# A graph-attention layer with LayerNorm: two broadcasts and the means moved on TensorE, PSUM banks swapped, the prologue reordered

## The reference

```python
h = einsum('bnd,ade->bane', x, W);  th = tanh(h)
attn = th @ w_src + swap(th @ w_dst)            # a score for each pair of nodes and head
attn = where(attn >= 0, attn, 0.2 * attn)
attn = where(adj, attn, -999.0);  attn = softmax(attn)
feat = elu(merge_heads(attn @ h + b))
gate = sigmoid(x @ H_w.T + H_b)
out = layernorm(x + gate * feat + (1 - gate) * x)
```

## Time and profile before

| | |
|---|---|
| median of 3 runs | 798.93 us (798.83 to 800.71) |
| the profiled execution | 799.27 us |
| its span in the trace | 797.5 us |
| PE busy | 724.3 us (91%) |
| DVE busy | 711.0 us (89%) |
| POOL busy | 536.8 us (67%) |
| ACT busy | 374.9 us (47%) |
| the chain that ended last | PE 89%, ACT 3%, DVE 3% |

### The profile page before, as it was taken

How to read it: one execution, slowest core, us unless ns; L and a number is a source line. 1 busy time by engine, 2 the same in 40 slices (tenths; PEclk the granted TensorE clock), 3 DMA queues, 4 the chain that set the end, 5 groups by cost and what they waited for, 6 DMA issues and landing times.

```text
span 797.5 us, 12614 instructions
## 1 busy us (share of the span) xinstructions
PE 724.3 (91%) x3472; PEld 401.5 (50%) x3472; DVE 711.0 (89%) x1277; ACT 374.9 (47%) x804; POOL 536.8 (67%) x380
## 2 busy tenths in 40 slices
PE   4299999999999999999999999999999999999970
PEld 4164564646456464645646454564545455553430
DVE  6668899989989998998999899898989999899885
ACT  4123426355553636555363645536264563626352
POOL 7964386775949677693957769395876939584500
PEclk9599999999999999999999999999999999999995
DMA  5020021112112111211211121211202121110202
GB/s 172 0 94 1 2 91 40 54 41 93 41 50 81 39 53 39 92 39 58 73 39 53 39 92 39 72 59 39 56 36 92 39 85 47 40 24 30 79 1 79
DMA packets 32875, 43.82 MB, mean 55 GB/s; under 512 B 1234, under 2 KB 26580, under 8 KB 32852
## 3 DMA queue, kind: packets, MB, share of 16 engines
q1 hardware_dynamic: 24660, 31.35, 12.5%
q10 hardware_dynamic: 8192, 12.19, 4.2%
HBM read 30.95 MB, written 12.58 MB: 55 GB/s over the span
## 4 chain that ended last, share of the span: by engine, by line
PE 89%; ACT 3%; DVE 3%; issue 2%; POOL 2%; DMA 1%; ACTq 0%; POOLq 0%; DVEq 0%; SPq 0%
PE out_T L798 47%; PE hg L726 27%; PE vb L782 7%; PE tr L806 6%; ACT att_T L400 1%; POOL th_w L257 1%; PE hg L767 1%; PE hg L772 1%; DMA ew<-in_W 1%; DVE ew L592 1%; DVE ex L684 0%; DMA out<-y 0%; PE hg L753 0%; ACT y L433 0%; DVE w_lo L510 0%
## 5 line engine op out<-in xcount | busy, mean ns | idle before, releaser
L592 DVE SCALAR_TENSOR_TENSOR ew<-vb,u,adj_in 128x512 f32<-128x512 f32 x768 | 536.1, 742 | 22.7 <-PE vb L782 22.7
L798 PE MATMUL out_T<-ew,vals 128*64 128x512 f32 x1536 | 392.3, 603 | 1.3 <-DVE ew L592 1.3
L257 POOL TENSOR_TENSOR th_w<-th,score_w 128x768 f32<-128x768 f32 x64 | 134.6, 2105 | 184.0 <-ACT th L371 147.9
L798 PEld LDWEIGHTS out_T<-ew,vals 128*64 128x64 f32 x1536 | 114.0, 136 | 200.6 <-issue 136.2
L400 ACT ACTIVATE att_T<-out_T,tiny 128x512 f32<-128x512 f32 x96 | 66.1, 689 | 245.7 <-PE out_T L798 245.7
L726 PE MATMUL hg<-w_hi,xT_hi 128*128 128x384 f32 x384 | 150.9, 393 | 14.4 <-DVE xT_lo L515 10.4
L726 PE MATMUL hg<-w_lo,xT_hi 128*128 128x384 f32 x384 | 130.2, 339 | 0.0
L726 PE MATMUL hg<-w_hi,xT_lo 128*128 128x384 f32 x384 | 88.5, 338 | 0.0
L726 PEld LDWEIGHTS hg<-w_hi,xT_hi 128*128 128x128 f32 x384 | 74.0, 193 | 25.2 <-issue 23.7
L806 PE MATMUL tr<-ident,att_T 128*128 128x128 f32 x384 | 59.1, 277 | 21.6 <-ACT att_T L400 21.6
L782 PE MATMUL vb<-v_T,head_sel 128*128 128x512 bf16 x192 | 74.4, 390 | 0.7 <-ACT v_T L392 0.7
(11 more groups left out here) (94 smaller groups left out, 718.8 us busy)
## 6 DMA issues: line engine op xcount, KB each, us to landing
xT_in<-in_xT SPq DMA_DIRECT2D x16, 768.0 KB, 4.6
x_in<-in_x SPq DMA_DIRECT2D x16, 768.0 KB, 4.5
out<-y ACTq DMA_DIRECT2D x15, 768.0 KB, 3.5
adj_in<-in_adjT SPq DMA_DIRECT2D x16, 256.0 KB, 4.8
ew<-in_W SPq DMA_DIRECT2D x1, 576.0 KB, 4.2
ew<-in_HwT SPq DMA_DIRECT2D x1, 576.0 KB, 8.0
score_w<-in_w_rows SPq DMA_DIRECT2D x1, 384.0 KB, 6.8
out<-y SPq DMA_DIRECT2D x1, 384.0 KB, 2.5
```

Source lines behind the costliest of these rows:

```text
L257: g.tensor_tensor(th_w[:, c % 2], th[:, c].unsqueeze(1).broadcast_to([P, 2, D]), score_w[:], ALU.mult).then_inc(S["thw_done"], 1)
L592: ve.scalar_tensor_tensor(out=ew[:, (2 * C * j + i) % SLOTS, :], in0=VB[h % 4][:], scalar=u[:, q, c, h:h + 1], in1=adj_in[:, q, c, :], op0 ...
L798: te.matmul(OUT[VW * k:VW * k + VW, :], vals[:, q, c, h, :], ew[:, t % SLOTS, :], start=(c == 0), stop=(c == C - 1)).then_inc(S["ew_free"], 1)
```

## The change

- On PE, the broadcasts of the heads 0 and 1 of the next batch leave attend 5 and stand ahead of it, behind transpose_out 4. Its eight matmuls stand together.
- The means of batch b move from the next step to the turn of the step, between transpose_v(b+1) and transpose_out 4, and wait for the last gate of b. In the last step they stand there too.
- On ACT, `copy_out(b, 4)` comes ahead of `copy_vT(b+1)`.
- The banks of HG are swapped: features 0 to 2 and gate 0 use HG[0], features 3, the other gates and the means HG[1]. The waits that guard them follow.
- ACT makes the tanh first and then the copy; what waits for a free bank now waits for the copy.
- In every product, the three high-by-high matmuls come first, then the three high-by-low, then the three low-by-high (before, the first two kinds took turns).
- Prologue: the products of batch 0 wait for each part when it is used, not for all at the start. DVE does its own weighing for batch 0. The zeros of `vals` are halved between DVE (at its start) and POOL. POOL does add_bias, then split_low of batch 1, then values, and then the two sums of `add_rows`, which were a part of `add_bias`.

```diff
@@ banks
-        G_BANK = [HG[1], HG[0], HG[1], HG[1]]
+        G_BANK = [HG[0], HG[1], HG[1], HG[1]]
-        mean_ps = HG[0][:, 0:D]
+        mean_ps = HG[1][:, 0:D]
-            return HG[0] if c == 3 else HG[1]
+            return HG[1] if c == 3 else HG[0]
@@ POOL before()
+                g.memset(vals[:, 1], 0.0).then_inc(S["pool_setup"], 1)
                 pool.wait_ge(S["pool_setup"], SETUP)
-                pool.wait_ge(S["ld_cols"], 16)
-                for c in range(C):
-                    weigh(0, c)
-                add_bias(0, 0)
+                add_bias(0)
+                for c in range(C):
+                    split_low(1, 1, c)
+                pool.wait_ge(S["dve_setup"], DVE_SETUP)
                 values(0, 0)
-                for c in range(C):
-                    split_low(1, 1, c)
+                add_rows(0, 0)
@@ ACT features(b, c)
-                a.activation(h_sb[:, c], feature_bank(b, c)[:, 0:D], ACT.Copy).then_inc(S["hcopy_done"], 1)
+                if isinstance(b, int) and b == 1:
+                    act.wait_ge(S["hb_sum_done"], 1)
                 if not isinstance(b, int) or b:
                     act.wait_ge(S["thw_done"], C * (b - 1) + c + 1)
                 a.activation(th[:, c], feature_bank(b, c)[:, 0:D], ACT.Tanh).then_inc(S["th_done"], 1)
+                a.activation(h_sb[:, c], feature_bank(b, c)[:, 0:D], ACT.Copy).then_inc(S["hcopy_done"], 1)
@@ ACT step
+                copy_out(b, 4)
                 if not last:
                     copy_vT(b + 1, 1 - q)
-                copy_out(b, 4)
@@ DVE before()
+                ve.memset(vals[:, 0], 0.0).then_inc(S["dve_setup"], 1)
...
-                ve.memset(vals[:], 0.0).then_inc(S["dve_setup"], 1)
...
                 for c in range(C):
+                    dve.wait_ge(S["th_done"], c + 1)
+                    ve.tensor_tensor(th_w[:, c % 2], th[:, c].unsqueeze(1).broadcast_to([P, 2, D]), score_w[:],
+                                     ALU.mult).then_inc(S["thw_done"], 1)
                     head_sums(0, c)
@@ PE products
                 for k in range(KD):
-                    mms += [(xT_hi[:, q, k, n], w_hi[:, k, col:col + D]), (xT_hi[:, q, k, n], w_lo[:, k, col:col + D])]
+                    mms.append((xT_hi[:, q, k, n], w_hi[:, k, col:col + D]))
+                for k in range(KD):
+                    mms.append((xT_hi[:, q, k, n], w_lo[:, k, col:col + D]))
@@ PE features of batch 0
+                    products(feature_bank(b, c), q, c, 0, [],
+                             {KD: (S["w_lo_done"], 1), 2 * KD: (S["xlo_done"], c + 1)}).then_inc(S["h_done"], 1)
@@ PE step
-                if not first:
-                    pe.wait_ge(S["vT_done"], b + 1)
-                    means(b - 1, 1 - q)
...
                 if not last:
                     transpose_v(b + 1)
+                means(b, q)
                 transpose_out(b, 4)
-                attend(b, q, 5, last)
+                if not last:
+                    broadcast_v(b + 1, 1 - q, 0)
+                    broadcast_v(b + 1, 1 - q, 1)
+                attend(b, q, 5)
```

66 lines of the change are left out of this document (37 added, 29 removed).

## The result

| | before | after |
|---|---|---|
| median | 798.9 us (798.83 to 800.71) | 766.1 us (763.75 to 767.3, 4 runs) |
| ratio of the medians, with its 95% interval | | 0.9581 (0.9551 to 0.9611) |
| the profiled execution | 799.27 us | 764.97 us |
| its span | 797.5 us | 763.2 us |
| DVE busy | 711.0 us (89%) | 711.3 us (93%) |

The forecast of the median was 768.1. The two spans differ by 34.3 us, where 30.8 were forecast. DVE has as much work as before; only its waits have gone.

A forecast was written before the change was run, and what follows sets the result against it. PE and DVE, almost side by side and waiting for each other at the turn between steps, bound the kernel. Turns 25.7 us plus prologue 5.1 make 30.8 us, from 798.93 to a median of 768.1 us; range 761 to 780.

The forecast's parts named there:

- Attend 5 in one piece: Turn on PE: without broadcasts inside, attend 5 ends at 545.35 instead of 547.09, set by DVE's last block of weights.
- 1.74 us a turn: Turn between steps: PE, DVE and ACT all leave it 1.74 us earlier, making a step 44.55 us instead of 46.29.
- The last turn: Turn without features: DVE's 1.24 us wait goes, with the issue behind it 1.3 us.
- ACT's order, v_T in time: Turn on ACT: with pair 4 copied first, v_T is done at 540.87, before the broadcasts need it; slack 0.3 us.
- Rival 3: Turn: broadcasts 0 and 1 become late, attend 5 waits for v_T, a turn gives 0.85 us; 781.0 us, chance 0.07.
- Nothing for the means, the banks and the product: Steps: moved means, swapped HG banks and regrouped products neither gain nor cost time.
- Rival 4: All products: regrouping loses a shared stationary operand's benefit, each matmul pays; 803 us at 32 ns each, chance 0.03.
- DVE's other waits: Turn: DVE's broadcast wait goes, its wait for transpose 5 is 0.2 us; PE idles some 0.9 ahead of features 1.
- Prologue, scores: Batch 0 weighing on DVE: second th_w stands behind POOL's add_bias, last reduction at about 25.7, 2.0 us earlier.
- Rival 1: Prologue: no standstill between DVE and POOL, last reduction starts at 22.5; 764.8 us, chance 0.12.
- Prologue, features 1: PE's product follows the first broadcast by some 1.3 us instead of 4.42, as POOL's low parts come earlier; 3.1 us.
- Rival 2: Prologue gives nothing: POOL or DVE is so late that the 5.1 us goes; 773.2 us, chance 0.08.

The follow-up runs named there:

- e10: e8 with the first two parts of split_v one block of weights later on DVE; 752.4 us, 0.9413.
- e11: e10 with DVE's reciprocal and division of a pair one block of weights later in every row; 752.09 us, 0.9405.
- e2: Changed kernel with ACT's copy of v_T ahead of the copy of pair 4 again; 772.17 us, 0.9669.
- e5: Kernel before with only broadcasts 0 and 1 put ahead of attend 5; 778.57 us, 0.9737.
- e1: Changed kernel with broadcasts 0 and 1 put back into attend 5; 780.72 us, 0.9778.
- e3: Changed kernel with the means back in the next step, between broadcast 3 and features 1; 764.06 us, 0.9562.
- e8: Changed kernel with ACT's x_plus moved behind features 1; 762.36 us, 0.9527.
- e6: Changed kernel with high-by-high and high-by-low matmuls taking turns again in every product; 766.91 us, 0.9573.
- e4: Changed kernel with the whole prologue of the kernel before, steps staying changed; 773.49 us, 0.9677.
- e7: Changed kernel with only the weighing of batch 0 back on POOL, ahead of add_bias; 767.04 us, 0.9579.

## Why the prediction was right, step by step

- **Attend 5 in one piece.** Right in kind and place. Its end comes 5.78 us after attend 4's (predicted 5.89). The last block ended at 517.45 + 0.66 + 0.74 = 518.85 and PE was through 1.07 later (predicted 1.04), so the bound was the one that I took, DVE's. e10 and e11 show the other bound: with DVE earlier, the end comes after 5.65. The two lie only 0.13 us apart. For the upper end of the range I had put PE's bound at 545.0, where the text before it has 545.15; so that end was some 2 us too high, which decides nothing.
- **1.74 us a turn was 1.88.** The term of the sum that was mis-sized, by 0.14. Of this 0.11 lie before attend 5's end, and the rest in ACT's way to features 1 (3.24 instead of 3.28). I took DVE's row of blocks from before as it stood, and it held a small delay: from the five blocks at 538.42 to the three at 542.91 there were 4.49 us, in after the same way takes 4.35 (513.10 to 517.45). The delay is the reciprocal's wait for transpose 4, which comes 1.66 us after attend 4's end in before and 0.93 in after. e2 and e5 put the transpose at 1.66 again, e2 by nothing but ACT's order, and the same way takes 4.48 us in both; in e1, e3, e8 and e10, with the transpose at 0.92 to 0.97, it takes 4.35 or 4.36. Fourteen turns make 2.0 us of the 3.5 that lie between the two spans' difference (34.3) and the forecast (30.8).
- **The last turn.** From attend 4's end to the second half of attend 1 it took 18.95 us and now takes 17.51: 1.44, predicted 1.3. The turns together give 27.8 by the rest of the sum, predicted 25.7.
- **ACT's order, v_T in time.** v_T follows att_T without a wait and PE has no wait for it ahead of the broadcasts. Rival 3 (781.0) falls. ACT started v_T 0.76 us after attend 4's end, where I had reckoned 0.81. Its slack was as reckoned, 0.3 us: v_T is done at 515.49, and by DVE's bound the broadcasts could have started as late as 515.8. e2 gives the price of the other order, 0.50 us a step.
- **Nothing for the means, the banks and the product.** Right: e3 and e6 have steps of 44.40 like after, and e5 with none of them has the step of e2 (the banks only together with the rest). Rival 4 (803) falls.
- **DVE's other waits.** 0.20 us for transpose 5 was predicted and found. PE idles 0.63 ahead of features 1 where I expected some 0.9; e8 puts 0.19 us on it, so it was no cover for anything large.
- **Prologue, scores: 2.0 us was 2.5.** Right that a th_w stands behind add_bias; but the third, not the second. Two moments were off: add_bias starts at 18.32, not near 17.5, and DVE starts at 14.74, not 16.1. I took 2.03 us for the subtraction of the bias from the earlier trace rows, and that row was itself a standstill behind POOL's weighing at 20.44 to 22.47; alone it takes 0.55. I had named this mechanism for the row at 8.35 and did not look for it in the next row. The sum to 25.7 was also short: it has 0.97 us each for the third and fourth th_w, a low part of x, and leaves out their own 0.91; with both it is 27.5. The fourth one measured 1.71. So that this term came within 0.5 us is in part luck, as DVE's late start stands against the early add_bias and the missing work. Rival 1 (no standstill) is refuted by the rows of 4.10 and 3.20 us, though by the number alone its 764.8 lies nearer to the result (1.3 us) than the forecast (2.0).
- **Prologue, features 1: 3.1 us was 3.5.** The product follows the first broadcast by 0.90 instead of 1.3: it starts beside the last broadcast. Rival 2 falls with e4, where the old prologue costs 7.4 us by the medians and 6.5 by attend 0.
- **What I had not reckoned:** 0.47 us on the way from the product to attend 0 (5.57 us, before 6.04), where PE's granted clock is 1.00 from 34.3 on. In before it is 0.50 between 36 and 40. In e6's trace it is not 1.00 either, and attend 0 comes 1.8 us later. I had no term for the clock, and it moves the result by nearly as much as the whole scores term. By place: 2.55 up to the first broadcast, 3.52 from there to the product, 0.47 from there to attend 0, together 6.54 where 5.1 were forecast.

The Trainium skill, page "SBUF — State Buffer", section "Who interferes with whom", stood in the prediction for the standstill. The traces agree: a th_w with two SBUF inputs takes 0.95 us alone and 3.20 to 4.10 when it comes during POOL's 3.42. They add that with POOL's work in pieces of 1.1 to 1.5 us the stand is 0.7 to 0.8 each time, but more of the th_w meet one.

## What to carry to other kernels

Where a pair of matmuls runs side by side in the array, keep the whole row of them together and put what others wait for ahead of it; but first find who sets the row's end, since another engine's last block may make it come no sooner. Before taking a duration from a row for a place that has changed neighbours, ask what else ran beside it there: the same subtraction took 0.55 and 2.03 us. And look for the queue that a moved piece of work leaves, as well as the one that it joins: with the weighing on POOL the scores came 2.5 us earlier than on DVE, and all of that was lost again behind POOL's queue. A wait in a prologue can cost twice: in e7 PE's clock was at half behind the standstill of 3.34 us.

## What the runs showed of the hardware that was not expected

- **Cut pairs.** Attend 5 with two broadcasts inside took 5.38 us by the starts (e1 and before); the two broadcasts and then the whole attend took 524.22 - 520.11 = 4.11 in e2. So the cuts alone cost 1.27 us. DVE was not what it waited for: in before, its last block was ready at 544.31, 2.8 us ahead of the end. The pieces tell more. The first cut comes after the third of eight matmuls, inside a pair, the second after the sixth, between pairs. The timeline of before, PE, has the start of the last piece, whose end is at 547.09:

```profile
546.08 1.08 PE L798 MATMUL out_T<-ew,vals 128*64 128x512 f32 x4
```

This whole pair took 1.01 us, and the first piece, a pair and one matmul, 1.86 (541.71 to 543.57), about twice the 0.90 that a pair takes in an attend without cuts (3.58 / 4). So a matmul left alone took about as long as a pair. Some 0.9 of the 1.27 us are the split pair; no run makes one of the two cuts alone.
- **A race of tenths.** The order in which DVE's third th_w and POOL's add_bias start, 0.09 us one way or 0.14 the other, moved the last reduction by 1.6 to 1.9 us. It differs between traces of the same prologue, and either engine may be the one that stands (POOL 4.14 instead of 3.42 us, DVE 4.10 or 3.74 instead of 0.95).
- **A clock that differs between executions.** With nearly the same code and times, PE's granted clock between 34.3 and 40 us was 1.00 in one trace (after) and 0.50 in another (e6); attend 0 came 1.8 us later in that one. A step later on has 1.00 in both. In e7 it was 0.50 between 36 and 41.8 us, behind a standstill of 3.34 us, and cost 1.39 us ahead of attend 0 and 1.27 in it.
- **No reuse of a loaded operand.** Two fp32 matmuls with the same stationary operand side by side or apart: PE busy 43.77 us of 44.40 in both.
